# Attention: projections of two head groups and half of the values moved into the first slots, the stack by way of HBM, maxima turned on VectorE

## What is computed

```python
x   # (8, 512, 512), ctx (8, 512, 512); 16 heads of 32
Q = (layernorm(x) @ Wq.T + bq)            # (B, H, S, 32)
K = (ctx @ Wk.T + bk)
V = (ctx @ Wv.T + bv)
attn = softmax(einsum('bhqd,bhkd->bhqk', Q, K) / sqrt(32))
x = x + tanh(g_xattn) * (einsum('bhqk,bhkd->bhqd', attn, V) @ Wo.T + bo)

h = layernorm(x)                           # 4096 tokens
gates, ids = top_k(softmax(h @ Wr + br), 2)   # 8 experts, 615 tokens at most for each
y = sum over experts of gate * (silu(h[e] @ W1[e] + b1[e]) @ W2[e] + b2[e])
x = x + tanh(g_ffn) * y
```

## Time and profile before

| | |
|---|---|
| median of 3 runs | 1974.52 us (1974.37 to 1977.56) |
| the profiled execution | 1978.65 us, span 1976.7 us |
| TensorE busy | 1796.4 us (91%) |
| VectorE / ScalarE / GpSimd busy | 1169.9 / 780.4 / 525.1 us |
| attention, start of the first projection to the end of the loop over batches | about 28 to 990 us |

### The profile page before, as it was taken

The page is one execution under the profiler, slowest core; times in us unless marked ns, Lnnn a source line. Parts: engine busy times, 40 slices in busy tenths (PEclk is TensorE's granted clock), DMA queues, the critical chain, the costliest instruction groups (busy, mean ns, idle before and its releaser), DMA issues.

```text
span 1976.7 us, 31098 instructions
## 1 busy us (share of the span) xinstructions
PE 1796.4 (91%) x10854; PEld 923.7 (47%) x10854; DVE 1169.9 (59%) x2131; ACT 780.4 (39%) x1012; POOL 525.1 (27%) x523
## 2 busy tenths in 40 slices
PE   7999999999999999999910699999999999999996
PEld 4333242332423324243210466767676766666664
DVE  5776867768677686866588453535344453534330
ACT  5443534436344353544430252516162534435240
POOL 2413443243432424332151122121221211212101
PEclk9999999999999999999955799999999999999998
DMA  5213113140321412104040143433434342524211
GB/s 191 71 44 100 51 52 98 43 128 22 82 67 47 124 32 75 64 14 115 12 143 23 39 142 74 133 91 93 125 94 128 73 136 56 159 67 136 70 45 25
DMA packets 116958, 162.22 MB, mean 82 GB/s; under 512 B 45236, under 2 KB 63040, under 8 KB 112808
## 3 DMA queue, kind: packets, MB, share of 16 engines
q1 hardware_dynamic: 72488, 134.00, 21.2%
q0 software_dynamic: 44416, 27.50, 7.4%
HBM read 108.92 MB, written 26.85 MB: 69 GB/s over the span
## 4 chain that ended last, share of the span: by engine, by line
PE 80%; DVE 8%; SPq 4%; issue 2%; ACT 2%; DMA 1%; POOL 1%; DVEq 0%; ACTq 0%; POOLq 0%
PE psum L1474 21%; PE psum L1451 19%; PE psum L1167 8%; PE psum L1264 6%; PE psum L1271 6%; PE psum L1255 5%; PE psum L1245 4%; SPq L355 4%; PE psum L1364 4%; PE psum L1172 2%; PE psum L1282 2%; DVE mx L843 1%; ACT osum L729 1%; PE psum L1427 1%; DVE cmp L989 1%
## 5 line engine op out<-in xcount | busy, mean ns | idle before, releaser
L1474 PE MATMUL psum<-w,hT 128*123 128x512 f16 x1920 | 420.3, 379 | 0.0
L843 DVE TENSOR_REDUCE mx<-psum 128x1 f32<-128x512 f32 x512 | 329.0, 684 | 152.0 <-PE psum L1245 150.8
L1451 PE MATMUL psum<-xgT,w 128*128 128x308 f16 (+1 forms) x3072 | 411.3, 294 | 0.7 <-DVE xgT L1098 0.7
L1451 PEld LDWEIGHTS psum<-xgT,w 128*128 128x128 f16 x3072 | 298.3, 97 | 109.8 <-DVE xgT L1098 0.8
L1474 PEld LDWEIGHTS psum<-w,hT 128*123 128x123 f16 x1920 | 257.9, 135 | 148.8
L721 ACT ACTIVATE pt<-psum 128x1024 f32<-128x1024 f32 x256 | 259.1, 1021 | 171.4 <-PE psum L1255 171.4
L771 ACT ACTIVATE h<-psum,b1c 128x308 f32<-128x308 f32 (+1 forms) x256 | 117.9, 511 | 378.1 <-PE psum L1451 377.3
L641 POOL DMA_INDIRECT out_dram<-y,idx_now x40 | 99.6, 2489 | 499.0 <-DVE y L1151 255.9
L1116 DVE TENSOR_TENSOR hT<-h,hT 128x615 f16<-128x615 f32 x128 | 102.5, 801 | 212.2 <-ACT hT L774 212.1
L1245 PE MATMUL psum<-stk 96*128 96x512 f16 x512 | 173.1, 384 | 33.8 <-DVE mx L843 14.3
L1167 PE MATMUL psum<-actT,wT 128*128 128x512 f16 x768 | 167.1, 379 | 2.0 <-DVE wT L830 2.0
(11 more groups left out here) (183 smaller groups left out, 1738.6 us busy)
## 6 DMA issues: line engine op xcount, KB each, us to landing
stage<-in_L_ffn_W_dram SPq DMA_DIRECT2D x64, 1024.0 KB, 5.2
stk<-qks SPq DMA_DIRECT2D x120, 96.0 KB, 2.6
xin<-in_x_dram SPq DMA_DIRECT2D x8, 1024.0 KB, 5.3
cin<-in_ctx_dram SPq DMA_DIRECT2D x8, 1024.0 KB, 5.5
xres<-in_x_dram SPq DMA_DIRECT2D x8, 1024.0 KB, 5.6
out_dram<-xres SPq DMA_DIRECT2D x32, 256.0 KB, 2.1
x_split<-x2hl SPq DMA_DIRECT2D x32, 256.0 KB, 2.2
stk<-qks POOLq DMA_DIRECT2D x72, 96.0 KB, 3.8
```

Source lines behind the costliest of these rows:

```text
L843: v.reduce_max(mx[:, KT * t + qt:KT * t + qt + 1], ps, AX.X).then_inc(read, 1)
L1451: mm = t_.matmul(psum[:, (2 * m + ch) % 4, 0:c1 - c0], w1[:, wp, kt, m * P:(m + 1) * P], xgT[:, xp, kt, c0:c1], start=(kt == 0 and (wp, xp ...
L1474: mm = t_.matmul(psum[0:CP, Y_BANK[c], :], hT[:, hp, k, c * CP:(c + 1) * CP], w2[:, wp, k, :], start=(k == 0 and (hp, wp) == (0, 0)), stop ...
```

## The change

It has three parts.

1. **Where the projections stand.** `QK_ORDER` becomes q0, k0, q1, k1, q2, k2, q3, k3. Ahead of slot 0 only the first four and the first two row tiles of V are computed (6 products of 12 matmuls in place of 8). Slots 0, 1, 3, 4 take one of q2, k2, q3, k3 each, slot 5 the other two tiles of V, whole instead of in halves. The router's `parts` stay in slot 4, its `logits` move to slot 5. Banks 3 and 5, unused in these slots before, are used too.
2. **The stack by way of HBM.** For each projection SP stores both halves (128 x 2 x 512, 256 KB) to a scratch tensor `qk_rows` in HBM, waits until they have landed, and then loads them with three transfers, each with the 32-row pieces of all four heads of the group (32 x 4 x 512, 128 KB). That is 8 x (1 + 3) = 32 transfers a batch on SP, and none on GpSimd, in place of 39 and 9. TensorE waits at slots 0, 4, 8 and 12 for the stack of that slot's group.
3. **The maxima turned on VectorE.** The transposition on TensorE goes. VectorE splits the 16 columns of maxima where they are (two operations of 128x16), then turns 32x32 blocks of them (128x32), and SP moves the result by four transfers instead of two. The store of the previous batch's rows and the load of `xres` move from behind group 0's maxima to behind group 1's.

The diff, cut to its core:

```diff
 
-SP_HEADS, POOL_HEADS = (0,), (1, 2, 3)
...
-QK_ORDER = [("q", 0), ("k", 0), ("q", 1), ("q", 2), ("q", 3), ("k", 1), ("k", 2), ("k", 3)]
+QK_ORDER = [("q", 0), ("k", 0), ("q", 1), ("k", 1), ("q", 2), ("k", 2), ("q", 3), ("k", 3)]
 UNITS = 4 * NG
 LAG_B, LAG_C = 6, 7
 SLOTS = UNITS + LAG_C
 LN_SLOT = LAG_B
-V_HALF = ((0, 0), (1, 1), (3, 3), (4, 5))
-V_SLOT = [last for _, last in V_HALF]
-X2T_SLOT, LG_SLOT = 2, 4
+QK_FIRST, QK_SLOT = 4, (0, 1, 3, 4)
+V_FIRST, V_SLOT = 2, (5, 5)
+X2T_SLOT, PARTS_SLOT, LG_SLOT = 2, 4, 5
+STORE_GROUP = 1
 GROUP_END = [LAG_C + 4 * g + 3 for g in range(NG)]
 GROUP_NORM = [t + 3 if t < UNITS else min(t + 2, SLOTS) for t in GROUP_END]
+
+
+def later_qk(s):
+
+    return [QK_FIRST + j for j, slot in enumerate(QK_SLOT) if slot == s]
+
+
+def later_v(s):
+
+    return [V_FIRST + j for j, slot in enumerate(V_SLOT) if slot == s]
...
@@ on SP @@
-        def stack_heads(eng, n, m0, m1, signal, heads=range(4)):
-
-
-            for j in heads:
-                for rows, part in enumerate(ROWS[n]):
-                    src = qks[32 * j:32 * j + 32, n, ("hi", "lo").index(part), m0:m1, :]
-                    dst = stk[32 * rows:32 * rows + 32, n, 4 * m0 + j:4 * (m1 - 1) + j + 1:4, :]
-                    eng.dma_start(dst, src).then_inc(signal[j], 16)
+        def stack_heads(eng, b, i):
+
+            which, m = QK_ORDER[i]
+            n = "qk".index(which)
+            eng.wait_ge(qk_split, NQ * b + i + 1)
+            eng.dma_start(qk_rows[n, m].rearrange("w p s -> p w s"), qks[:, n, :, m, :]).then_inc(qk_out[i], 16)
+            eng.wait_ge(qk_out[i], 16 * b + 16)
+            for rows, part in enumerate(ROWS[n]):
+                src = qk_rows[n, m, ("hi", "lo").index(part)].rearrange("(j d) s -> d j s", j=4)
+                eng.dma_start(stk[32 * rows:32 * rows + 32, n, 4 * m:4 * m + 4, :], src).then_inc(stk_in[m], 16)
 
         def heads_stacked(eng, n):
 
-            eng.wait_ge(stk_q0, 12 * 16 * n)
-            for j in range(4):
-                eng.wait_ge(stk_k0[j], 3 * 16 * n)
-            eng.wait_ge(stk_rest, (12 + 3 * len(SP_HEADS)) * 16 * n)
-            eng.wait_ge(stk_rest_pool, 3 * len(POOL_HEADS) * 16 * n)
+            for i in range(NQ):
+                eng.wait_ge(qk_out[i], 16 * n)
 
...
-                sp.wait_ge(qk_split, NQ * b + 1)
-                stack_heads(sp, 0, 0, 1, [stk_q0] * 4)
-                sp.wait_ge(qk_split, NQ * b + 2)
-                stack_heads(sp, 1, 0, 1, stk_k0)
-                sp.wait_ge(qk_split, NQ * b + 5)
-                stack_heads(sp, 0, 1, KT, [stk_rest] * 4)
-                sp.wait_ge(qk_split, NQ * b + 8)
-                stack_heads(sp, 1, 1, KT, [stk_rest] * 4, SP_HEADS)
+                for i in range(QK_FIRST + 2):
+                    stack_heads(sp, b, i)
                 for g in range(NG):
 
-                    copied(sp, use, ("mT", g), b)
-                    for part in range(2):
-                        dst = stk[96 + part:97 + part, 0, 4 * g:4 * g + 4, :].rearrange("o h (t q) -> o (h t) q", q=P)
-                        sp.dma_start(dst, mrow[:, g, part, :]).then_inc(mrow_in[g], 16)
+                    sp.wait_ge(mrow_ready, NG * b + g + 1)
+                    rows = stk[96:98, 0, 4 * g:4 * g + 4, :].rearrange("o h (t a q) -> o (h t) a q", t=KT, a=4)
+                    for a in range(4):
+                        sp.dma_start(rows[:, :, a, :], mrow[32 * a:32 * a + 32, g, :]).then_inc(mrow_in[g], 16)
                     if g == 0:
+                        for i in range(QK_FIRST + 2, NQ):
+                            stack_heads(sp, b, i)
+                    if g == STORE_GROUP:
                         if not first:
                             store_rows(b)
...
@@ on VectorE @@
                     maxima(t, (0, 1))
                     if t % 4 == 0 and 4 <= t <= UNITS:
                         g = t // 4 - 1
-                        ps, read = filled(dve, use, ("mT", g), b)
-
-                        dve.wait_ge(mrow_in[g], 32 * b)
-                        v.tensor_scalar(mrow[:, g, 0, :], ps[0:16, 0:P], -1.0 / SQ ** 2, None, ALU.mult).then_inc(mrow_hi, 1)
-                        dve.wait_ge(mrow_hi, NG * b + g + 1)
-                        v.scalar_tensor_tensor(mrow[:, g, 1, :], ps[0:16, 0:P], -1.0 / SQ ** 2, mrow[:, g, 0, :],
-                                               ALU.mult, ALU.subtract).then_inc(read, 1)
-                    maxima(t, (2, 3) if t % 4 else (3, 2))
+                        for qt in (2, 3):
+                            copied(dve, use, ("S", 4 * g + 3, qt), b)
+                        best = mx[:, 16 * g:16 * g + 16]
+                        v.tensor_scalar(mhl[:, g, 0:16], best, -1.0 / SQ ** 2, None, ALU.mult).then_inc(max_hi, 1)
+                        dve.wait_ge(max_hi, NG * b + g + 1)
+                        v.scalar_tensor_tensor(mhl[:, g, 16:32], best, -1.0 / SQ ** 2, mhl[:, g, 0:16],
+                                               ALU.mult, ALU.subtract).then_inc(max_split, 1)
+                        dve.wait_ge(max_split, NG * b + g + 1)
+
+                        dve.wait_ge(mrow_in[g], 64 * b)
+                        v.transpose(mrow[:, g, :], mhl[:, g, :]).then_inc(mrow_ready, 1)
+                    maxima(t, (2, 3))
...
@@ on TensorE @@
-                def values(tt, half):
-
-                    if half == 0:
-                        claim(pe, use, ("v", tt), b)
-                    bank, _ = use(("v", tt), b)
-                    for kt in (2 * half, 2 * half + 1):
-                        for xp, wp in PARTS:
-                            last = t_.matmul(psum[:, bank, :], actT[:, 1, xp, kt, tt * P:(tt + 1) * P], wT[:, 2, wp, kt, :],
-                                             start=(kt == 0 and (xp, wp) == (0, 0)),
-                                             stop=(kt == KT - 1 and (xp, wp) == (1, 0)))
-                    if half == 1:
-                        last.then_inc(bank_full[bank], 1)
-
+                def values(tt):
+
+                    dst, full = claim(pe, use, ("v", tt), b)
+                    product(dst, [(actT[:, 1, xp, kt, tt * P:(tt + 1) * P], wT[:, 2, wp, kt, :])
+                                  for kt in range(KT) for xp, wp in PARTS]).then_inc(full, 1)
+
+                for i in range(QK_FIRST):
+                    queries_keys(i)
+                for tt in range(V_FIRST):
+                    values(tt)
                 if first:
                     pe.wait_ge(k_ones, 1)
                 for s in range(SLOTS):
 
-                    if s == 0:
-                        pe.wait_ge(stk_q0, 12 * 16 * b + 12 * 16)
-                    if s < 4:
-                        pe.wait_ge(stk_k0[s], 3 * 16 * b + 3 * 16)
-                    if s == 4:
-                        dmas = (12 + 3 * len(SP_HEADS)) * 16
-                        pe.wait_ge(stk_rest, dmas * b + dmas)
-                        dmas = 3 * len(POOL_HEADS) * 16
-                        pe.wait_ge(stk_rest_pool, dmas * b + dmas)
+                    if s % 4 == 0 and s < UNITS:
+                        pe.wait_ge(stk_in[s // 4], 96 * b + 96)
                     scores(s, 0)
                     scores(s, 1)
+                    for i in later_qk(s):
+                        queries_keys(i)
                     if s == X2T_SLOT:
                         rows()
-                    for tt in range(KT):
-                        if s in V_HALF[tt]:
-                            values(tt, V_HALF[tt].index(s))
+                    if s == PARTS_SLOT:
+                        parts()
+                    for tt in later_v(s):
+                        values(tt)
                     if s == LG_SLOT:
-                        parts()
+                        logits()
                     u = s - LAG_B
+                    if u == 0:
+
+                        copied(pe, use, ("v", 3), b)
+                        copied(pe, use, ("qk", 7), b)
                     if 0 <= u < UNITS and u % 4 == 0:
-                        pe.wait_ge(mrow_in[u // 4], 32 * b + 32)
+                        pe.wait_ge(mrow_in[u // 4], 64 * b + 64)
                     less_maxima(u, 0)
...
-                    if s % 4 == 0 and 4 <= s <= UNITS:
-                        g = s // 4 - 1
-
-                        for qt in (2, 3):
-                            copied(pe, use, ("S", 4 * g + 3, qt), b)
-                        dst, full = claim(pe, use, ("mT", g), b)
-                        t_.transpose(dst[0:16, 0:P], mx[:, 16 * g:16 * g + 16], ident[:, :]).then_inc(full, 1)
                     if not last_batch and s == UNITS:
                         for i in act_tiles(s):
                             inputs_transposed(b + 1, i // KT, i % KT)
-                    if s % 4 == 0:
-
-                        less_maxima(u, 1)
-                        scores(s, 3)
-                        scores(s, 2)
-                    else:
-                        scores(s, 2)
-                        less_maxima(u, 1)
```

(34 more changed lines are left out.)

44 lines of the change are left out of this document (28 added, 16 removed).

## The result

The changed kernel takes 2018.65 us (median of 4 runs, 2013.51 to 2023.37), the one before 1976.04 in the same sessions: ratio 1.0214, 95% interval 1.0185 to 1.0243. It is 2.1% slower, where 1.3% (2001 us, range to 2018) was forecast. The direction and most of the places were right; the loss is 42.6 us where 26.1 were forecast.

The account below looks back on a forecast made before the run. The prediction took TensorE, busy 91% of the span, as the bound. Its terms, 19.0 - 13.7 + 17.2 + 3.6 = +26.1 us on the profiled 1978.65, gave 2004.8, as a median 2001 us (1.3% slower), range 1977 to 2018.

Parts of the forecast that it names:

- runs of four score blocks: Ends of slots 0 to 5: four blocks together six times instead of two, 1.14 us each, +4.56 us a batch.
- router's transposes, maxima: Transposes lose a bank wait, -0.31 us; maxima in slots 4, 8, 12, 16 save 0.86, 0.35, 0.55, 0.11 a batch.
- wait at slot 4 gone: TensorE no longer waits there for the last transfer into the stack: -13.7 us over seven batches.
- wait at slot 0: TensorE waits 2.45 us for group 0's stack through HBM in seven batches: +17.2 us.
- Other things moved ... All at nothing: Later stacks, the later store and `xres` load, and GpSimd's dropped transfers were all claimed to cost nothing.
- The prediction's bound for the three operations: VectorE's split and turn of the maxima: from nothing up to +21 us; about 0.5 us beside TensorE's work was taken.
- The clock: Two falls at slot 4 go, -3.6 us; falls behind slot 0 in four of seven batches, +7.2; net +3.6 us.
- The estimate that the prediction sets beside this chain: Slot 0's stores and loads through HBM: 2.6 us a store, 2.3 a load, so a wait of 3.35 us.
- the late maxima: Rival: transfers of maxima come too late, three groups wait 0.5 to 1 us each, about +18 us, 2019; 5%.
- the hidden wait: Rival: TensorE finds the stack ready at slot 0 and the clock does not fall, +1.7 us, 1976; 7%.
- the slow HBM: Rival: the wait at slot 0 is 5 us, the clock falls in all seven batches, +49 us, 2024; 14%.
- the free score blocks: Rival: four score blocks together cost nothing new after a whole projection, -10.4 us, 1964; 8%.

Follow-up runs that it names:

- run 1: Changed kernel with moved Q and K products, router's transposes and last tile of V halved, between and behind the score-block pairs: 1953.53 us, ratio 0.9881.
- run 4: Kernel before with the whole tile of V between the two pairs of score blocks in slots 0, 1 and 3: 1991.90 us, ratio 1.0078.
- run 6: Kernel before with only the maxima split and turned on VectorE, four transfers, and score blocks ordered 2, 3 in every slot: 1968.95 us, ratio 0.9957.
- run 5: Kernel before with only the stack through HBM, all eight projections still ahead of the slots: 1966.01 us, ratio 0.9946.
- run 8: Changed kernel with three tiles of V ahead of slot 0 instead of two, only the fourth in slot 5: 1999.26 us, ratio 1.0111.
- run 2: Changed kernel with the store of the previous rows and the load of `xres` back behind the first group's maxima: 2000.27 us, ratio 1.0121.
- run 9: Changed kernel with GpSimd's four additions to `xres` behind its work for the first head group, store and load staying late: 1998.78 us, ratio 1.0120.
- run 3: Changed kernel with the router's logits ahead of the two tiles of V in slot 5 instead of behind them: 2006.47 us, ratio 1.0151.
- the combined one: Changed kernel with halved products, store and `xres` load back behind the first group, three tiles of V ahead of slot 0: 1942.61 us, ratio 0.9830.
- run 10: As the combined one, but only x's rows stored behind the first group's maxima, the router's rows behind the second's: 1935.69 us, ratio 0.9796.

## Why the prediction was right or wrong

Per batch at full clock, forecast against measured; the last column is the run that shows it:

| term | forecast | measured | shown by |
|---|---|---|---|
| runs of four score blocks | +4.56 | 4 x 1.13 in the timeline; 6.1 for all six against halves | timeline; runs 1 and 4 |
| router's transposes, maxima | -2.18 | about -2 in place (a difference, not seen by itself); maxima alone -1.2 for -1.87 in the kernel before | run 6 |
| wait at slot 4 gone | -1.96 | -1.2 to -1.6 alone | run 5 |
| wait at slot 0 | +2.45 | +1.8 | waits; run 8 |
| VectorE's split and GpSimd's additions | 0 | +1.1 (seven batches) | runs 2 and 9 |
| sum | +2.9 | +3.1 to +3.7 | batches |

**The step that failed** is "Other things moved ... All at nothing". The load of `xres` was checked against group 0's normalisation in slot 13, called its first reader. It is not: GpSimd's four additions read `xres` first, and they stood waiting for this load (4.39 us in the row above). What they would run beside was not asked. In the fourth batch they moved from slot 11 and the start of slot 12, where they were done before the split of that slot, to slot 12 and the start of slot 13, and the change had just replaced two operations of VectorE with PSUM inputs by ones that read only SBUF. This costs 1.1 us in each of seven batches, 8 in all. The Trainium skill has the rule (SBUF — State Buffer, Who interferes with whom): VectorE and GpSimd share a pair of ports to SBUF, held by one of them at a time, and an operation of VectorE with two SBUF inputs contends with one of GpSimd that reads SBUF. The trace agrees: 1.20 us against 0.176, with GpSimd's additions at 1.24. That the PSUM inputs mattered is on record as well. In the last batch of the kernel before, the old operations ran beside the same additions and took what they always take:

```profile
922.87 0.28 DVE L864 TENSOR_SCALAR mrow<-psum 16x128 f16<-16x128 f32 x1 [0.56 <-PE psum L1336]
923.18 0.28 DVE L866 SCALAR_TENSOR_TENSOR mrow<-psum,mrow 16x128 f16<-16x128 f32 x1
```

```profile
922.24 2.50 POOL L541 TENSOR_TENSOR xres<-xres,tgbo 128x512 f32<-128x512 f32 x2 [24.73 <-DMA xres<-in_x_dram]
```

At the same place of run 6 the new ones, on SBUF, took 0.79 and 1.20. The prediction's bound for the three operations, up to 21 us, held the cost, but the value inside it was taken from their width.

**The clock** was the second step that failed, and about as large: right that it matters, wrong in where. Net +3.6 us were forecast, for falls at slot 0. They came at the end of slot 5, behind the logits and a run of four, in four to six batches at about 3 us instead of 1.8; less the 3.6 of before that is +8 to +14. Run 3 shows that the logits' place matters, runs 2, 8 and 9 that the clock falls at the same place in only one or two batches when the batch is otherwise 1 to 1.6 us shorter. Why it does is open: these runs change spacing and idle time together, and each has one profile.

**The wait at slot 0** was overpriced by 0.65 us a batch, 4.6 in all, mostly since the issue time was taken from transfers within SBUF (0.59 each), and it is 0.43. This hid part of the other two misses. The estimate that the prediction sets beside this chain, from the page DMA: Bandwidth & Descriptors of the Trainium skill, is there for transfers that GpSimd issues. SP's, here, landed in 2.5 us in the median, stores and loads alike.

Of the rivals, the late maxima did not come in the changed kernel, though the combined one had them for another reason, the store ahead of them; the hidden wait and the slow HBM are refuted by the mean wait of 1.8 us; the free score blocks by runs 1 and 4. Worked out in full for the two profiled executions: 26 us for the eight batches at full clock (1.9 for the first, which meets neither the wait at slot 0 nor the collision, some 3.4 for each of the others), 11 net for the clock (four falls at 3.0, one at slot 0 at 1.7, 1.6 at the start, less two of 2.0 before), and 2.6 ahead of and behind the batches, which were not looked into. That is the 39.5 us between them. Between the medians it is 42.6; how many falls the other executions had no run shows.

## What to carry to other kernels

Where an engine fills two buffers and another empties them more slowly, it matters between which pairs the other work stands, not how much there is: the same products cost some 49 us more whole, in one place, than cut in halves and set between all pairs. When a transfer is moved, look for its true first reader, at what it then does, and beside which operations of the other engines; two small operations of VectorE that lost their PSUM input took up to 1.2 us more beside GpSimd's additions. And try the parts of a change one by one: parts 2 and 3 of this one were worth 10 and 7 us, while with part 1's order put right (run 1) the whole change is a gain of 1.2%.

## What the runs showed of the hardware

- A SCALAR_TENSOR_TENSOR of 128x16 with both inputs in SBUF took up to 1.21 us beside GpSimd's additions (run 3) and 0.176 without. A TENSOR_SCALAR of the same size, with a single SBUF input, took up to 1.30 beside them (run 1) and 1.11 beside GpSimd's subtraction (run 10, in slot 4 of every batch of the loop, where TensorE shows no wait for it). The same two operations reading PSUM took 0.28 beside additions (kernel before, last batch).
- Three loads of 128 KB from HBM were issued in 1.28 us by SP and landed in 2.5 (median), the stores of 256 KB in 2.5 as well. In the kernel before, the 32 and 96 KB pieces within SBUF took 0.59 us each (median) to issue.
- The clock held through 13 of the 14 waits of 1.6 to 2.0 us at slot 0 (this kernel, two executions), and fell, for about 7 us, at the end of slot 5 behind 1 us of matmuls of 8 columns and a run of four that loses 1.14.
